# A recurrent gate and a 32-expert feed-forward layer on one core: stores among loads, one statistics call per step, and a fifth set of result buffers

## The chip, the cores and the metric
The kernel runs on one core of a Trainium2 chip. The metric is the device time of one execution in microseconds, lower being better; given is the median of several executions. The profile and the trace come from one further execution with the hardware profiler on.

## The reference, cut to what matters
x is 4 x 2048 tokens of 256 numbers, so 8192 tokens.

```python
xn = layernorm(x)
# s: recurrent layer of xn
combined = xn @ W_in + b_in               # 256 embedding columns, 8 state inputs
gate = sigmoid(combined @ W_g + b_g)      # 8 gates per token
state[t] = gate[t] * state[t-1] + (1 - gate[t]) * state_in[t]      # a scan along 2048 tokens
s = concat(embed, states) @ W_out + b_out
# y: 32 experts, each token goes to 4 of them, at most 1280 tokens each
scores = softmax(xn @ wg.T)               # 8 groups of 4 experts, 4 groups kept, then the top 4
y[token] += weight * ((silu(xe @ w1) * (xe @ w3)) @ w2)            # for each expert's tokens xe
# z: one expert that all tokens go through
z = (silu(xn @ sw1) * (xn @ sw3)) @ sw2
out = x + s * silu(y + z)
```

## The kernel before
**Units of work.** The tokens are 64 tiles of 128. A pair is two tiles (256 rows), the unit in which every matrix product is done. A group is two pairs (four tiles, 512 tokens), the unit of the loads of x, of the layer norm's statistics and of the routing. There are 32 pairs and 16 groups.

**First stage, 32 steps p = 0 to 31.** A step works on one pair. PE's loop is at L1174: it turns the next pair's rows (`transposes`, L1056), multiplies the pair by the shared expert's first matrix, then does `meanwhile` (L1180 to L1200), then the third matrix. `meanwhile` adds the states' part of s (`add_states`, L1135), forms the gates' input of the next pair (`gate_inputs(p + 1)`, L1145 to L1158), which needs the low halves `xl` of that pair from DVE (L1698, waited for at L1148), places a group's rows (`positions`), finishes the pair before (`down(p - 1)`, L1090 to L1092, its result is z), and forms the state's inputs and the logits (`s_inputs(p + 1)`, L1123 to L1125). In step 29 it also counts the early rows (`cnt_early`, L1196 to L1200).

DVE's loop is at L1891. A step is, in this order: `gate_act(p-1)` (L1704), `xlow(p+1)` (L1698, which `gate_inputs(p + 1)` waits for), `act_low` (L1708); then in even steps the end of the routing of the group before, the recurrence of the next pair (`recurrence`, L1713 and L1721; it waits for ACT's tanh of the gate inputs), `states_low` (L1727, waits for ACT's `states_high`, L1448), `statistics`, and the routing's begin; in odd steps `statistics`, the recurrence, the group's routing (top groups, top experts) and `states_low`. `statistics(g)` (L1601) is four BN statistics instructions (L1607) and four aggregates (L1610). Calls of the early steps: group 3 in step 0 and group 4 behind its states, groups 5 and 6 behind the states of step 2 (L1917 to L1919), group 7 at the end of step 3 (L1949 to L1951), group g + 6 ahead of the recurrence of step 2g + 1 for g = 2 to 9.

ACT copies z out of PSUM into a single buffer `yw` (`take_z`, L1424 to L1431) and waits for the store of the z before (L1430). It comes before the next `states_high` and before the normalised rows of the next tiles in ACT's order.

POOL's order (L895 to L903): for each of the 16 groups, once `dest_idx` (DVE, L1817) is there, 16 indirect DMAs that scatter rows of x with their routing weights to `slot_rows`, the expert's table in DRAM (L900). Behind all of them come the adds (L883): two indirect DMAs per pair that add an expert's results to `y_sum` (z's table in DRAM).

SP's order is written out by hand (L529 to L840). Loads of x by group: 0 to 5 early, 6 to 9, then 10 to 15 (L558 and L559), each with a wait for the load eight groups before; behind all of these a loop that stores z of pairs 0 to 29 (L561 to L568), then the early experts' rows (`load_early`, L673), which need the counts of L1199 and the scatters up to a group.

**Expert stage.** 142 pairs q, PE some 4.7 us each. Experts 0 to 5 start early with 17 pairs while the last groups are still being routed; from expert 6 on each has a section of four pairs and, where it has over 1024 rows, a fifth (DVE's `section`, L2022). A result, scaled by its weight, is written by DVE (`take_y_before`, L1969 to L1978) to a result buffer and added by POOL. A set is five buffers; there are four sets, A to D, carved from the storage of x and others (L203 to L208), used in turn by `y_set` (L229 to L231). Before DVE writes to a buffer it waits until the add that used it has landed: `free_wait` (L2008) for slots 0 to 3, and for a fifth result the sum of all fifths of experts up to two before (L2031). x, whose storage the sets took, is loaded again between the sections (`load_x_again`, L667, L757 to L772), for the last stage, which computes `out`.

DVE runs the sections of experts 6 to 9 as straight code, those of 10 to 17 as two turns of a loop of four sections (L2063 to L2069), 18 and 19 straight, the rest as a loop of two. POOL's code has the same form (L978 to L990).

Of the kernel before, what the change touches and what calls it, by code (L numbers as in the profile page):

```python
# [8 lines left out]
U32 = mybir.dt.uint32  # L9
# [5 lines left out]
D = 256  # L15
# [8 lines left out]
E = 32  # L24
# [40 lines left out]
SETS = 4  # L65
CYCLE_END = 18
# [15 lines left out]
def build(nc, x, w_in, b_in, w_g, b_g, w_out, b_out, wg, w1, w2, w3, sw1, sw2, sw3, out):  # L82
    ctx = ExitStack()
    with ctx:
# [120 lines left out]
        y_idx_early = x_space(2 * (2 * SET + EXTRA_Y)).bitcast(U32)  # L205
        assert words[0] <= X_KEPT * CHUNK * D
        y_flat += [x_words[:, c * CHUNK * D:(c + 1) * CHUNK * D] for c in range(X_KEPT, X_KEPT + SET)]
        y_flat += set_c + set_d + extra_y  # L208
# [10 lines left out]
        SET_A, SET_B, SET_C, SET_D, EXTRA = (n * SET for n in range(SETS + 1))  # L219
# [122 lines left out]
        added = [[sem(f"added{n}_{slot}") for slot in range(PAIRS)] for n in range(SETS)]  # L342
# [99 lines left out]
        def set_uses(e):  # L442

            return (e - FIRST) // SETS if e < CYCLE_END else (e - CYCLE_END) // 2 + (CYCLE_END - FIRST) // SETS

# [74 lines left out]
        def _(sp):  # L520
# [38 lines left out]
            for g in range(10, GROUPS):  # L559
                load_x(g)  # L560
# [6 lines left out]
            with sp.Fori(0, A_PAIRS - 2) as q:  # L567
                store_z(q)  # L568
# [105 lines left out]
            for q in range(2):  # L674
                load_early(q)
            sp.wait_ge(xn_ready, N // P - 2 * GT)
# [83 lines left out]
            sp.wait_ge(first_added, first_adds(CYCLE_END - 6))  # L760
            with sp.Fori(CYCLE_END, CYCLE_END + 4) as e:
                section(e)
                load_x_again(e - FIRST)
            sp.wait_ge(first_added, first_adds(CYCLE_END + 1))
            with sp.Fori(CYCLE_END + 4, CYCLE_END + 9) as e:
                section(e)
                for n in range(2):
                    load_x_again(e * 2 - (CYCLE_END + 4) * 2 + CYCLE_END + 4 - FIRST + n)
            section(CYCLE_END + 9)
            load_x_again(X_KEPT - 1)  # L770
            with sp.Fori(CYCLE_END + 10, E - 2) as e:
                section(e)  # L772
# [71 lines left out]
        def _(pool):  # L844
# [133 lines left out]
            for e in range(FIRST, FIRST + SETS):  # L978
                section(e, y_set(e), y_set(e - 1) if e > FIRST else None, set_uses(e - 1) + 1)
            with pool.Fori(0, (CYCLE_END - FIRST) // SETS - 1) as i:  # L980
                for n in range(SETS):
                    section(i * SETS + FIRST + SETS + n, n * SET, (n - 1) % SETS * SET, i + 1 if n == 0 else i + 2)
            for e in range(CYCLE_END, CYCLE_END + 2):
                section(e, y_set(e), y_set(e - 1), set_uses(e - 1) + 1)
            with pool.Fori(0, (E - 2 - CYCLE_END - 2) // 2) as i:
                section(i * 2 + CYCLE_END + 2, SET_B, SET_A, i + 4)
# [23 lines left out]
        def _(pe):  # L1010
# [163 lines left out]
            for p in range(A_PAIRS):  # L1174
# [5 lines left out]
                def meanwhile():  # L1180
                    add_states(p, i)
                    if has_next:
# [13 lines left out]
                    if p == A_PAIRS - 3:  # L1196
                        pe.wait_ge(early_seen, GROUPS - 2)
                        pe.wait_ge(pos_taken, GROUPS - 2)
                        mm(cnt_early, ones[:, 0:1], seen_early[:, 1:GROUPS - 1, :].rearrange("p g e -> p (g e)"),  # L1199
                           start=True, stop=True).then_inc(cnt_ready, 1)  # L1200
# [373 lines left out]
        def _(ve):  # L1574
# [316 lines left out]
            for p in range(A_PAIRS):  # L1891
# [13 lines left out]
                if i == 0:  # L1905
# [24 lines left out]
                else:  # L1930
# [3 lines left out]
                    if p == A_PAIRS - 3:  # L1934
                        count_early()
                        mark_late()
                    if has_next:
                        if 2 <= g < 10:
# [3 lines left out]
                        recurrence(p + 1, 1 - i, g % BATCH_GROUPS == BATCH_GROUPS - 1)  # L1942
                    if has_next:
# [189 lines left out]
```

## Time and profile before

| | |
|---|---|
| median of 3 runs | 1074.14 us (1073.2 to 1076.17) |
| the profiled execution | 1077.56 us |
| its span, first to last instruction | 1075.8 us |
| mean granted clock of PE | 0.972 |
| PE / DVE / ACT / POOL busy | 93% / 72% / 51% / 68% |

The share of busy time is a mean over stages. The stages lie, in the profiled execution, at 0 to 102.6 us (set-up and the first groups), to 404 us (the rest of the first stage and the early experts beside the scatters), to 510.4 us (early experts and expert 6 to 8 beside the adds), to 1000 us (the other experts), and to 1075.8 us (the rows beyond the sections and `out`). "PEclk" is the granted clock of PE: 1.00 is 2.4 GHz, 0.50 is 1.2 GHz.

### The profile page before, as it was taken

How to read it: one execution, taken by the hardware profiler on the slowest of the kernel's cores; microseconds unless marked ns; L12 is line 12 of the kernel's file. 1: busy time of each engine (PE TensorE's matmuls, PEld its weight loads, DVE VectorE, ACT ScalarE, POOL GpSimd, SP SyncE). 2: the span in 40 equal slices, each digit the busy share in tenths (PEclk: the TensorE clock that was granted, in tenths of full speed). 3: DMA queues.
4: the chain of work that ended last, by engine and by line, in shares of the span. 5: the costliest groups of instructions: out<-in, count | busy, mean ns of one | idle time of the engine just before them, and what ended most of it. 6: DMA issues, size and time to landing. Idle time of an engine off the chain costs nothing.

```text
span 1075.8 us, 29677 instructions
## 1 busy us (share of the span) xinstructions
PE 1001.6 (93%) x8031; PEld 955.9 (89%) x8031; DVE 775.6 (72%) x2475; ACT 549.5 (51%) x1039; POOL 726.3 (68%) x572
## 2 busy tenths in 40 slices
PE   7879999998979997997999999999999999999965
PEld 6878898888879997997999999999999999999822
DVE  6778898887868874765677667767667777767674
ACT  4657786877654442443344344444444444444444
POOL 3066777777777776777888887666666666665440
PEclk8889999999999999999999999999999999999997
DMA  9933433443357878997899988988788988878879
GB/s 257 285 120 130 145 141 141 143 145 140 141 159 250 261 230 169 207 181 144 161 174 201 191 167 170 199 184 179 168 201 184 211 191 190 170 141 179 217 204 340
DMA packets 179346, 199.28 MB, mean 185 GB/s; under 512 B 20737, under 2 KB 171058, under 8 KB 179250
## 3 DMA queue, kind: packets, MB, share of 16 engines
q1 hardware_dynamic: 124992, 126.70, 39.6%
q0 software_dynamic: 53664, 71.50, 35.0%
q8 instruction: 34, 0.56, 0.2%
q14 instruction: 62, 0.51, 0.2%
q10 hardware_dynamic: 594, 0.01, 0.0%
HBM read 96.89 MB, written 104.90 MB: 188 GB/s over the span
## 4 chain that ended last, share of the span: by engine, by line
PE 55%; POOL 19%; issue 12%; DMA 6%; DVE 3%; ACT 2%; SPq 1%; POOLq 1%; DVEq 0%; ACTq 0%
POOL slot_rows L900 16%; PE h L1072 10%; PE h L1074 10%; PE h L1073 10%; PE yb L1090 5%; PE yb L1092 5%; PE yb L1091 5%; PE xt L1056 5%; POOL y_sum L883 4%; DMA y_sum<-y_more,y_idx 2%; DMA x_all<-slot_rows 1%; DMA y_sum<-x_all 1%; DMA y_sum<-yw,y_idx 1%; DVE s_all L2103 1%; DMA w_hl<-y_sum 1%
## 5 line engine op out<-in xcount | busy, mean ns | idle before, releaser
L1072 PE MATMUL h<-xh,w_hl 128*128 (+1 forms) x1392 | 410.4, 295 | 3.6 <-DVE xl L1698 2.0
L1074 PE MATMUL h<-xl,w_hl 128*128 (+1 forms) x1392 | 393.5, 283 | 0.0
L1073 PE MATMUL h<-xh,w_hl 128*128 (+1 forms) x1392 | 392.1, 282 | 0.0
L1422 ACT ACTIVATE acth<-act 128x512 fp32r<-128x512 f32 x174 | 109.9, 632 | 346.3 <-PE yb L1092 306.0
L1072 PEld LDWEIGHTS h<-xh,w_hl 128*128 128x128 f32 x1392 | 264.0, 190 | 5.5 <-issue 5.0
L1073 PEld LDWEIGHTS h<-xh,w_hl 128*128 128x128 f32 x1392 | 264.3, 190 | 0.0
L1074 PEld LDWEIGHTS h<-xl,w_hl 128*128 128x128 f32 x1392 | 263.5, 189 | 0.0
L1708 DVE TENSOR_TENSOR actl<-act,acth 128x512 fp32r<-128x512 f32 x174 | 120.6, 693 | 173.7 <-ACT acth L1422 173.2
L1090 PE MATMUL yb<-w_hl,acth 128*128 128x256 f32 x692 | 199.7, 289 | 8.6 <-DVE x_all L1977 6.3
L883 POOL DMA_INDIRECT y_sum<-x_all,y_idx x98 | 156.0, 1592 | 69.1 <-DVE x_all L1977 42.2
L1092 PE MATMUL yb<-w_hl,actl 128*128 128x256 f32 x692 | 197.5, 285 | 0.0
L1091 PE MATMUL yb<-w_hl,acth 128*128 128x256 f32 x692 | 197.1, 285 | 0.0
L900 POOL DMA_INDIRECT slot_rows<-rows,dest_idx x128 | 130.3, 1018 | 86.4 <-DVE dest_idx L1817 48.3
L883 POOL DMA_INDIRECT y_sum<-y_more,y_idx x82 | 130.5, 1592 | 59.8 <-DVE y_more L1977 32.5
L900 POOL DMA_INDIRECT slot_rows<-x_all x128 | 132.5, 1035 | 39.0 <-issue 38.4
L883 POOL DMA_INDIRECT y_sum<-x_all x78 | 124.6, 1597 | 33.3 <-issue 17.2
L1090 PEld LDWEIGHTS yb<-w_hl,acth 128*128 128x128 f32 x692 | 132.9, 192 | 15.4 <-issue 15.3
L1416 ACT ACTIVATE act<-h 128x512 f32<-128x512 f32 x174 | 104.1, 599 | 81.0 <-DVE actl L1708 76.8
L1698 DVE TENSOR_TENSOR xl<-xt,xh 128x512 f32 (+1 forms) x174 | 119.1, 685 | 20.3 <-ACT xh L1410 18.0
L1092 PEld LDWEIGHTS yb<-w_hl,actl 128*128 128x128 f32 x692 | 133.1, 192 | 0.0
L1091 PEld LDWEIGHTS yb<-w_hl,acth 128*128 128x128 f32 x692 | 132.8, 192 | 0.0
L1704 DVE TENSOR_TENSOR act<-act,h 128x512 f32<-128x512 f32 x174 | 117.8, 677 | 3.9 <-PE h L1074 3.0
(253 smaller groups left out, 1606.0 us busy)
## 6 DMA issues: line engine op xcount, KB each, us to landing
rows<-slot_rows SPq DMA_DIRECT2D x122, 289.0 KB, 4.2
raw<-L_ffn_w SPq DMA_DIRECT2D x99, 256.0 KB
slot_rows<-rows SPq DMA_DIRECT2D x32, 289.0 KB
x_all<-L_attn_x SPq DMA_DIRECT2D x16, 512.0 KB, 9.3
x_all<-L_attn_x SPq DMA_DIRECT2D x32, 256.0 KB
out<-s_all SPq DMA_DIRECT2D x32, 256.0 KB, 3.7
y_sum<-yw SPq DMA_DIRECT2D x31, 256.0 KB
x_all<-slot_rows SPq DMA_DIRECT2D x20, 289.0 KB, 4.5
```

The source lines that it names most:

```text
L883: pool.indirect_dma_start(y_dram, bass.IndirectOffsetOnAxis(y_index(buf, t), 0), y_out[buf][:, t, :], None, bounds_check=token_bound, oob_ ...
L900: pool.indirect_dma_start(slot_table, bass.IndirectOffsetOnAxis(dest_idx[slot][:, t, k:k + 1], 0), rows[slot][:, t, :], None, bounds_check ...
L1072: mm(out, high, xh[:, k, cols], start=(k == 0), stop=False)
L1073: mm(out, low, xh[:, k, cols], start=False, stop=False)
L1074: ins = mm(out, high, xl[:, k, cols], start=False, stop=(k == KD - 1))
L1090: mm(dst, acth[:, c:c + P], wts[:, 4, k, :], start=(k == 0), stop=False)
L1091: mm(dst, acth[:, c:c + P], wts[:, 5, k, :], start=False, stop=False)
L1092: ins = mm(dst, actl[:, c:c + P], wts[:, 4, k, :], start=False, stop=(k == KD - 1))
L1422: av(acth[:, :], act[:, :], ACT.Copy).then_inc(acth_ready, 2)
L1698: v.tensor_tensor(xl[:, :, cols], xt[:, :].rearrange("p (k t) -> p k t", k=KD), xh[:, :, cols].bitcast(F32), ALU.subtract).then_inc(xl_rea ...
L1704: v.tensor_tensor(act[:, :], act[:, :], h3[:, :], ALU.mult).then_inc(act_ready, 1)
L1708: v.tensor_tensor(actl[:, :], act[:, :], acth[:, :].bitcast(F32), ALU.subtract).then_inc(actl_ready, 2)
```

## The change
1. **SP.** The stores of z(0), z(1) and z(2) are put ahead of the loads of x of groups 10, 12 and 14. `load_early(0)` comes ahead of the store of z(28), `load_early(1)` ahead of that of z(29).
2. **DVE, statistics.** One call per step: group 4 in step 0 as before, group 5 in step 1 ahead of `recurrence(2)`, group 6 in step 2, group 7 in step 3 ahead of `recurrence(4)`.
3. **Step 29.** DVE's `count_early` and `mark_late` move behind `recurrence(30)`; PE's `cnt_early` moves from the end of `meanwhile` to right behind `add_states`.
4. **Result buffers.** A fifth set, E, of five buffers in the storage of x's chunks 0 to 4, used by expert 7 alone, which waits for no add. Experts 8 to 19 go round B, C, D, A; from 20 on B and A in turn, as before. One more primer DMA (a 16th) runs at POOL's start.
5. **Loops and loads.** Experts 6 to 11 are straight code, 12 to 19 two turns of a loop of four, 20 and 21 straight, then a loop of two. x's chunks 5 to 12 are loaded again behind sections 6 to 13, chunks 0 to 4 behind 14 to 18, 13 to 15 behind 19 to 21, then two each.

```diff
-SETS = 4
-CYCLE_END = 18
+SETS = 5
+CYCLE = 4
+CYCLE_START = 8
+CYCLE_END = 20
+KEPT_START = 14
...
-            return (SET_A, SET_B, SET_C, SET_D)[(e - FIRST) % SETS] if e < CYCLE_END else (SET_B, SET_A)[e % 2]
+            if e < CYCLE_START:
+                return (SET_A, SET_E)[e - FIRST]
+            return CYCLE_SETS[(e - CYCLE_START) % CYCLE] if e < CYCLE_END else (SET_B, SET_A)[e % 2]
...
-            for g in range(10, GROUPS):
-                load_x(g)
...
-            with sp.Fori(0, A_PAIRS - 2) as q:
+            for g in range(10, GROUPS):
+                if g % 2 == 0:
+                    store_z(g // 2 - 5)
+                load_x(g)
+            with sp.Fori(3, A_PAIRS - 4) as q:
                 store_z(q)
...
             for q in range(2):
                 load_early(q)
+                store_z(A_PAIRS - 4 + q)
...
-            with sp.Fori(FIRST, CYCLE_END) as e:
+            with sp.Fori(FIRST, KEPT_START) as e:
+                section(e)
+                load_x_again(e - FIRST + SET)
+            sp.wait_ge(first_added, first_adds(KEPT_START - SET))
+            with sp.Fori(KEPT_START, KEPT_START + SET) as e:
+                section(e)
+                load_x_again(e - KEPT_START)
...
                 def meanwhile():
                     add_states(p, i)
+                    if p == A_PAIRS - 3:
+                        pe.wait_ge(early_seen, GROUPS - 2)
+                        pe.wait_ge(pos_taken, GROUPS - 2)
+                        mm(cnt_early, ones[:, 0:1], seen_early[:, 1:GROUPS - 1, :].rearrange("p g e -> p (g e)"),
+                           start=True, stop=True).then_inc(cnt_ready, 1)
...
-                    if g == 0:
-                        statistics(4)
-                    if g == 1:
-                        statistics(5)
-                        statistics(6)
+                    if g in (0, 1):
+                        statistics(4 + 2 * g)
...
-                    if p == A_PAIRS - 3:
-                        count_early()
-                        mark_late()
                     if has_next:
+                        if g in (0, 1):
+                            statistics(5 + 2 * g)
...
                         recurrence(p + 1, 1 - i, g % BATCH_GROUPS == BATCH_GROUPS - 1)
+                    if p == A_PAIRS - 3:
+                        count_early()
+                        mark_late()
...
                     if g == 1:
-                        statistics(7)
                         variances(norm_chunk(g + 3))
...
-                if e < FIRST + SETS:
+                if e == FIRST + 1:
+                    return None, 0
+                if e < CYCLE_START + CYCLE - 1:
```

## Rows read from the trace of the kernel before

**Rows 1.** The page: busy time by engine, then the chain that ended last by engine.
```profile
PE 1001.6 (93%) x8031; PEld 955.9 (89%) x8031; DVE 775.6 (72%) x2475; ACT 549.5 (51%) x1039; POOL 726.3 (68%) x572
PE 55%; POOL 19%; issue 12%; DMA 6%; DVE 3%; ACT 2%; SPq 1%; POOLq 1%; DVEq 0%; ACTq 0%
```

**Rows 2.** Windows: us, sum, busy PE, PEld, DVE, ACT, POOL, PEclk, DMA, GB/s.
```profile
102.60:404.00 301.40, 283.23 (x2353) 268.11 (x2350) 244.88 (x1007) 199.33 (x398) 232.88 (x225) 0.99 0.52 172
404.00:510.40 106.40, 93.78 (x777) 93.01 (x777) 64.80 (x169) 40.05 (x71) 77.29 (x48) 0.97 0.87 176
510.40:1000.00 489.60, 487.42 (x4103) 486.81 (x4104) 347.03 (x894) 215.57 (x383) 350.64 (x221) 0.99 0.86 180
```

**Rows 3.** Timeline of POOL: start, duration, instruction, idle time before it and releaser.
```profile
50.64 1.25 POOL L900 DMA_INDIRECT slot_rows<-rows,dest_idx  x1 [38.89 <-DVE dest_idx L1817]
...
77.32 1.29 POOL L900 DMA_INDIRECT slot_rows<-rows,dest_idx  x1 [6.10 <-DVE dest_idx L1817]
...
101.32 0.98 POOL L900 DMA_INDIRECT slot_rows<-rows,dest_idx  x1 [3.34 <-DVE dest_idx L1817]
...
398.95 1.07 POOL L900 DMA_INDIRECT slot_rows<-x_all  x1 [0.30 <-issue]
...
504.92 1.55 POOL L883 DMA_INDIRECT y_sum<-y_more,y_idx  x1 [0.30 <-issue]
```

**Rows 4.** Groups of POOL's instructions from 102.6 to 400.1 us, by line.
```profile
L900 POOL DMA_INDIRECT slot_rows<-x_all x128 | 132.5, 1035 | 39.0 <-issue 38.4 <-DVE x_all L1817 0.3 <-DVE x_all L1977 0.3
```

**Rows 5.** Timeline of PE after 400 us, then of DVE at 509 us.
```profile
408.94 1.12 PE L1056 MATMUL xt<-ident,x_all 128*128 128x128 f32 x4 [5.20 <-DMA x_all<-slot_rows]
...
510.33 0.55 PE L1090 MATMUL yb<-w_hl,acth 128*128 128x256 f32 x1 [6.27 <-DVE x_all L1977]
...
509.00 0.15 DVE L1976 CAST x_all<-meta 128x1 uint32 x1 [6.68 <-DMA y_sum<-y_more,y_idx]
```

**Rows 6.** Timeline of PE: the end of down(1), then the gate inputs of three early steps.
```profile
50.98 0.41 PE L1092 MATMUL yb<-w_hl,actl 128*128 128x256 f32 x1
...
60.41 0.37 PE L1155 MATMUL gb<-xh,wgh 128*48 128x256 f32 x1 [2.83 <-issue]
...
73.07 0.29 PE L1155 MATMUL gb<-xh,wgh 128*48 128x256 f32 x1 [3.72 <-issue]
...
93.12 0.29 PE L1155 MATMUL gb<-xh,wgh 128*48 128x256 f32 x1 [0.85 <-DVE xl L1698]
```

**Rows 7.** Timeline of DVE, 39 to 77 us, in order of time.
```profile
39.54 0.41 DVE L1713 SCALAR_TENSOR_TENSOR raw<-raw,gb 16x256 f32<-16x256 f32 x1 [1.15 <-ACT raw L1442]
...
54.67 1.41 DVE L1607 BATCH_NORM_STATS2 stats<-x_all 128x6 f32<-128x256 f32 x4
...
56.60 1.41 DVE L1607 BATCH_NORM_STATS2 stats<-x_all 128x6 f32<-128x256 f32 x4
...
63.35 0.41 DVE L1713 SCALAR_TENSOR_TENSOR raw<-raw,gb 16x256 f32<-16x256 f32 x1 [2.14 <-ACT raw L1442]
...
67.73 0.41 DVE L1727 TENSOR_TENSOR state_hl<-raw,state_hl 16x256 fp32r<-16x256 f32 x1 [1.03 <-ACT state_hl L1448]
...
69.62 1.40 DVE L1607 BATCH_NORM_STATS2 stats<-x_all 128x6 f32<-128x256 f32 x4
```

**Rows 8.** Windows of the early steps, columns as in rows 2.
```profile
60.40:63.90 3.50, 3.49 (x17) 3.42 (x18) 1.11 (x3) 2.86 (x6) 2.58 (x4) 0.51 0.31 110
74.10:80.90 6.80, 6.80 (x41) 6.58 (x41) 3.75 (x16) 3.09 (x7) 2.97 (x3) 0.50 0.23 77
82.00:100.00 18.00, 16.98 (x144) 15.91 (x143) 15.14 (x67) 14.05 (x29) 12.32 (x13) 1.00 0.39 140
```

**Rows 9.** Timeline of ACT, then of SP's queue, at the second copy of z.
```profile
52.81 0.60 ACT L1431 ACTIVATE yw<-yb 128x512 f32<-128x512 f32 x1 [3.78 <-DMA y_sum<-yw]
...
47.31 18.14 SPq L564 DMA_DIRECT2D y_sum<-yw  x3
```

**Rows 10.** Timeline of DVE behind the end of its loop of four sections.
```profile
617.99 0.20 DVE L1966 COPY meta<-rows 128x66 f32 x1 [2.71 <-issue]
```

More of the change, by code:

```diff
@@ L217, in y_index @@
             return y_idx_early[:, column:column + 1]
-        SET_A, SET_B, SET_C, SET_D, EXTRA = (n * SET for n in range(SETS + 1))
+        SET_A, SET_B, SET_C, SET_D, SET_E, EXTRA = (n * SET for n in range(SETS + 1))
+        CYCLE_SETS = (SET_B, SET_C, SET_D, SET_A)
         BEHIND_FIFTH, BEHIND_LAST = EXTRA + 1, EXTRA + 2
@@ L341, in build @@
         y_ready = sem("y_ready")
-        added = [[sem(f"added{n}_{slot}") for slot in range(PAIRS)] for n in range(SETS)]
+        added = [[None] + [sem(f"added{n}_{slot}") for slot in range(1, PAIRS)] for n in range(SETS)]
         first_added = sem("first_added")
@@ L442, in set_uses @@
         def set_uses(e):
-            return (e - FIRST) // SETS if e < CYCLE_END else (e - CYCLE_END) // 2 + (CYCLE_END - FIRST) // SETS
+            if e < CYCLE_START:
+                return 0
+            if e < CYCLE_END:
+                return (e - CYCLE_START) // CYCLE + (y_set(e) == SET_A)
+            return (e - CYCLE_END) // 2 + (CYCLE_END - CYCLE_START) // CYCLE + e % 2
         def first_adds(e):
@@ L977, in _ @@
                 pool.reg_mov(fifth_behind, 1)
-            for e in range(FIRST, FIRST + SETS):
+            for e in range(FIRST, CYCLE_START + CYCLE):
                 section(e, y_set(e), y_set(e - 1) if e > FIRST else None, set_uses(e - 1) + 1)
-            with pool.Fori(0, (CYCLE_END - FIRST) // SETS - 1) as i:
-                for n in range(SETS):
-                    section(i * SETS + FIRST + SETS + n, n * SET, (n - 1) % SETS * SET, i + 1 if n == 0 else i + 2)
+            with pool.Fori(0, (CYCLE_END - CYCLE_START) // CYCLE - 1) as i:
+                for n in range(CYCLE):
+                    section(i * CYCLE + CYCLE_START + CYCLE + n, CYCLE_SETS[n], CYCLE_SETS[n - 1], i + 2)
             for e in range(CYCLE_END, CYCLE_END + 2):
@@ L1195, in meanwhile @@
                         positions(g - 1)
-                    if p == A_PAIRS - 3:
[L1197 to L1200, printed above, removed]
                 up(p, w_hl[1], region(i), meanwhile)
@@ L2028, in body @@
                     if slot == PAIRS:
-                        if isinstance(e, int) and e < FIRST + SETS:
+                        if isinstance(e, int) and e < CYCLE_START + CYCLE - 1 and e != FIRST + 1:
                             ve.wait_ge(*waits(slot))
@@ L2062, in _ @@
                 pair(PAIRS, 1, (FIRST - 2, SET_A + PAIRS, fifth_added, 32), slot=PAIRS)
-            for e in range(FIRST, FIRST + SETS):
+            for e in range(FIRST, CYCLE_START + CYCLE):
                 section(e, (e + 1) % 2, y_set(e), lambda slot, e=e: free_wait(e, slot), FIRST - 2 if e == FIRST else None)
-            with ve.Fori(0, (CYCLE_END - FIRST) // SETS - 1) as i:
-                for n in range(SETS):
-                    e = i * SETS + FIRST + SETS + n
-                    section(e, (n + 1) % 2, n * SET, lambda slot, e=e, n=n: (first_added, first_adds(e - SETS))
-                            if slot == 0 else (added[n][slot], slot_adds(slot, i + 1)))
+            with ve.Fori(0, (CYCLE_END - CYCLE_START) // CYCLE - 1) as i:
+                for n, home in enumerate(CYCLE_SETS):
+                    e = i * CYCLE + CYCLE_START + CYCLE + n
+                    section(e, (n + 1) % 2, home, lambda slot, e=e, home=home: (first_added, first_adds(e - CYCLE))
+                            if slot == 0 else (added[home // SET][slot], slot_adds(slot, i + (2 if home == SET_A else 1))))
             for e in range(CYCLE_END, CYCLE_END + 2):
@@ L2075, in _ @@
                     section(e, 1 - n, home, lambda slot, e=e, home=home: (first_added, first_adds(e - 2)) if slot == 0 else
-                            (added[home // SET][slot], slot_adds(slot, i + 4)))
+                            (added[home // SET][slot], slot_adds(slot, i + (5 if home == SET_A else 4))))
             uses = set_uses(E - 1) + 1
```

24 lines of the change are left out of this document (10 added, 14 removed).

## The prediction

> **What bounds the kernel now.** I read the page first [rows 1]: PE is busy for 93% of the span, and on the chain that ended last PE has 55% and POOL 19%, nearly all of it scatters of one line. So there are two bounds, one after the other, and the windows by stage tell where. From 510.4 to 1000 us PE is busy for 487.42 of 489.6 us: nothing but PE's own work counts there. From 102.6 to 404 us it is busy for 283.23 of 301.4 us, and from 404 to 510.4 us for 93.78 of 106.4 us [rows 2]: there somebody else leads.
>
> That is POOL. Its timeline shows the scatters of group 0 from 50.64 us, of group 1 from 77.32 us, of group 2 from 101.32 us, each after an idle time that DVE's `dest_idx` ended (38.89, 6.10, 3.34 us); the last of group 15 begins at 398.95 us after an idle time of only 0.30 us [rows 3]. From group 2 on there are 14 groups of 16 scatters, 224 of them; at 1.035 us each [rows 4] and 0.30 us between them that is 299 us, and from 101.3 us to the last one's end at 400.0 us there are 298.7. So POOL doesn't pause once between group 2's dispatch and 400 us. The adds follow, and they too are back to back when the second half of a pair is added at 504.92 us [rows 3].
>
> Now who waits for POOL? PE, twice. At 408.94 us it has stood 5.20 us for a row load that needs the last scatter; at 510.33 us it has stood 6.27 us for DVE, which had stood 6.68 us for an add into `y_sum` (the one of 504.92 us), before it could take expert 8's fifth result [rows 5]. That is the wait of L2031, for all fifths of experts up to 6. Behind it PE never waits for POOL again. So the end is group 2's dispatch, plus POOL's fixed work to 508.8 us, plus PE's fixed work behind 510. What PE alone saves between 102 and 510 us makes those two waits longer and is given back; what brings group 2's dispatch forward passes to the end.
>
> **The change part by part.** *Statistics, the part that counts.* Up to 100 us, DVE's chain from the states through the routing decides. PE stands 2.83 us ahead of the gate inputs of pair 4 at 60.41 us and 3.72 us ahead of those of pair 5 at 73.07 us [rows 6], both times until DVE has made `xl`. In DVE's timeline [rows 7] the calls of groups 5 and 6 begin at 54.67 and 56.60 us, between the states and `xl`. One of them leaves: −1.93 us.
>
> The call of group 7 stands at 69.62 us, again between the states and `xl`: it leaves too, at the price of the other call, start to start: −1.93 us. Where it goes, ahead of `recurrence(4)`, DVE stands 2.14 us for ACT at 63.35 us [rows 7]; 1.93 us of work fit into that, so it costs nothing there. If that cover were gone, it would cost its 1.93 us.
>
> Between the two lies a wait of 1.03 us for ACT's high states at 67.73 us [rows 7], which come behind ACT's copy of z, hence behind PE's `down(2)`. PE does those products from 60.40 to 63.90 us at a granted clock of 0.51, the lower level of 1.2 GHz, right behind its idle time of 2.83 us [rows 8]. With 1.93 us less in front of it, that idle time is 0.9 us. The nearest row for such a short one is 93.12 us, 0.85 us idle [rows 6], and the clock of the window around it is 1.00 [rows 8]. At 2.4 GHz the 3.49 busy us take half, so the high states come up to 1.75 us earlier and the wait of 1.03 us nearly goes: I take −0.85, leaving the 0.2 us that DVE commonly waits for ACT; bounds −1.03 and 0.
>
> Against it: the call of group 5 goes into step 1, ahead of `recurrence(2)`, where DVE waits 1.15 us at 39.54 us [rows 7]: 1.93 − 1.15 = +0.78 us (bounds 0.78 and 1.93). That delay reaches the dispatch of group 0, where it costs nothing while group 1's comes 5 us earlier: POOL had 6.10 us to spare between the two [rows 3]. On the way to step 2 it meets the next part.
>
> *Stores of z among the loads.* ACT's second copy of z begins at 52.81 us, after 3.78 us in which it ended up waiting for the store of the first, which SP issued at 47.31 us [rows 9] behind six loads of x of 512 KB each; PE had finished `down(1)` at 51.39 us [rows 6]. DVE's states of step 2 wait for ACT behind that copy. With the store ahead of the loads the copy is released by PE: 51.39 + 0.78 = 52.17 us, 0.64 us before 52.81. So the +0.78 is swallowed here, and up to 0.64 us are won on top; bounds +0.78 (should the store be no earlier) and −0.64. I take −0.3 for both together, half of what is won, since DVE's other work of step 2 comes 0.78 us later too. The loads of groups 10 to 15 come later, but the statistics of group 10 are taken only in step 9, behind 100 us. SP stands at three stores instead of running through; behind it are those loads alone.
>
> Sum for group 2's dispatch: −1.93 − 1.93 − 0.85 − 0.3 = −5.0 us, so 101.32 becomes 96.3. Bounds: −3.86 + 0.78 = −3.1 with the 0.85 gone and the 0.78 kept, −3.86 − 1.03 − 0.64 = −5.5 with all at their best. Two things could cap it. POOL must be free: group 0's scatters begin at 50.64 + 0.78 and, like group 1's, take 101.32 − 3.34 − 77.32 = 20.7 us, so POOL is free for group 1 from 72.1 us, just before 77.32 − 5.0 = 72.3; that is over at 93.0 us, before 96.3. And steps 4 to 6 have to keep their length, since PE is busy for 16.98 of the 18 us from 82 to 100 us [rows 8]; I take them unchanged.
>
> *Step 29, early rows.* `cnt_early` without its wait behind `meanwhile`, and early rows ahead of the last stores, can save PE a few us before 404. POOL is scattering then without a pause, so I cost them at nothing: they lengthen the wait that stood at 408.94 us. If POOL weren't the bound there, they would add to the gain.
>
> *Fifth set.* The wait at 510.33 us is for the fifths' adds [rows 5], not for a set to come free; expert 8's fifth still waits so (L2031 is unchanged). From there on PE has 2.2 us of idle time in all of 489.6 us [rows 2], so buffers that come free earlier buy nothing: 0. The changed reloads of x run behind sections on SP in that same stretch; as long as PE stays full they cost nothing. If an add were late where a reload or a set waits, the wait would show in PE.
>
> *Loops.* DVE stood for 2.71 us with nothing that the profile shows [rows 10], behind the turn of its loop of four sections; the new code has one such turn too, two experts later: 0.
>
> In all −5.0 us: 1074.14 − 5.0 = **1069.1 us**. The rows come from an execution of 1077.56 us, 3.4 us above the median; the same difference would make a profiled execution of about 1072.5. The forecast's own range, by the bounds, is 1068.6 to 1071.0.
>
> **The rivals.** *R1, the clock gives more.* PE's idle time at pair 5's gate inputs doesn't vanish: `xl` comes 5.0 us earlier, PE's own work up to 4.0 us (1.93 and 0.3, and up to 1.75 from the clock), so of 3.72 us some 2.7 remain. In before, 3.72 us were followed by 6.80 us at 0.50 [rows 8], which cost PE half of that, 3.4 us. If the shorter stand isn't followed by a slow stretch, steps 4 to 6 shrink by 3.4, and the gain is 5.0 + 3.4 = 8.4, capped by POOL, which is free for group 2 at 93.0 + 0.3: 8.0, 1066.1 us. Against it: the 2.83 us at 60.41 were followed by a slow stretch.
> The Trainium skill ("TensorE: Matmul & The Clock Gate", Part 1: The HAM clock gate) says that the low clock is the state an idle engine falls into and that the same kernel shows 6, 11 or 14 slow matmuls from run to run; by that the time would be drawn between this rival and the forecast in each run. The one trace of before can't show it.
>
> *R2, the clock gives less.* The slow stretch behind pair 4's gate inputs stays in spite of the shorter idle time, and another of 3.4 us falls into steps 5 or 6: the sum is then −3.1 + 1.7 = −1.4, 1072.7 us (1071.0 to 1074.1). For it speaks that PE's short idle times are many; against it, the window at 1.00 around the 0.85 us.
>
> *R3, the fifth set removes the wait at 510.33.* Then 6.27 us more go, and with them the half-speed stretch that follows a long stand, some 2: 1074.1 − 5.0 − 6.3 − 2 = 1060.8 us. Against it is the releaser: an add into `y_sum` from `y_more` [rows 5], a set which E doesn't replace. That the change doesn't do what it says would look like this rival's opposite, and is the forecast without it.
>
> *R4, slower.* DVE's straight code now holds experts 10 and 11. If the branch over a fifth that isn't there stops DVE as its loop's turn does (2.71 us [rows 10]), PE, which has nothing in reserve behind 510, loses some 2 us and up to 1.7 by a slow stretch: 3.7 us each. Two such stops cost 7.4, the change ends at +2.4, 1076.5 us; it decides from the second stop on, and a third makes it 1080.2. Against it: the same branches lay inside the loop of before, and only its turn shows such an idle time.
> The Trainium skill ("Runtime: NRT & Kernel Launch", Instruction fetch mechanics) says that a taken branch to code that isn't held forces a fetch before execution goes on. The row of 2.71 us agrees; that a short forward branch does it no row here shows.
>
> **How the numbers follow.** Forecast 0.54, R1 0.18, R2 0.16, R3 0.04, R4 0.08. The range 1065.9 to 1072.8 takes the forecast with its bounds, nearly all of R1 and two thirds of R2: about 0.8. A measurement of this kernel can tell about 0.3% from no change, 3.2 us. Faster than 1070.9: forecast (less 0.02 at its upper bound), R1 and R3, 0.74; within: R2, that 0.02 and half of R4, 0.22; slower: the other half of R4, 0.04.
>
> **What would show it.** In the trace of after: POOL's first scatter of group 2 near 96.3 us and its last near 394.0; no idle time of PE over 1 us at pair 4's gate inputs, some 2.7 us at pair 5's; the two waits of rows 5 still there, the first one longer, the second one ending near 505.3 us; ACT's second copy of z released by PE. The prediction is wrong if group 2's dispatch moves by less than 3 us or more than 6, if the shift at group 2 isn't found again at 510 us, or if PE idles anew behind it.

## The result, and the profile after

The changed kernel takes 1068.19 us (median of 20 runs, 1063.86 to 1075.76) beside 1073.32 us for the kernel before (20 runs on the same chips): a ratio of 0.995 with a 95% interval of 0.9933 to 0.9966, so 5.1 us less. The forecast was 5.0 us less. The profiled execution has a span of 1069.6 us, 6.2 us under that of before.

First the page's busy times and the windows of the stages, here bounded by group 2's first scatter, the end of the last scatter and the end of PE's second stand (in rows 2 the middle bound, 404 us, lies 4 us behind the end of the last scatter). The columns are those of rows 2: us, sum, PE, PEld, DVE, ACT, POOL, PEclk, DMA, GB/s.

```profile
PE 997.1 (93%) x8031; PEld 952.3 (89%) x8031; DVE 774.9 (72%) x2475; ACT 548.9 (51%) x1039; POOL 726.4 (68%) x573
...
94.00:390.90 296.90, 282.80 (x2353) 268.17 (x2352) 245.34 (x1006) 199.20 (x398) 228.94 (x224) 0.99 0.53 173
390.90:504.30 113.40, 95.22 (x787) 94.24 (x786) 65.54 (x171) 40.64 (x72) 80.66 (x50) 0.95 0.85 168
504.30:1000.00 495.70, 491.61 (x4131) 490.61 (x4132) 350.02 (x903) 217.13 (x386) 354.01 (x222) 0.99 0.86 180
```

Little was saved in work: PE is busy for 997.1 us against 1001.6. In the last of these stretches PE is again busy all but 4 us. The change lies in when things begin. POOL's timeline (start, duration, instruction, idle time before and its releaser) answers to rows 3:

```profile
50.70 1.25 POOL L916 DMA_INDIRECT slot_rows<-rows,dest_idx  x1 [38.47 <-DVE dest_idx L1833]
...
71.97 0.98 POOL L916 DMA_INDIRECT slot_rows<-rows,dest_idx  x1 [0.30 <-issue]
...
93.97 0.98 POOL L916 DMA_INDIRECT slot_rows<-rows,dest_idx  x1 [0.80 <-DVE dest_idx L1833]
...
389.92 0.98 POOL L916 DMA_INDIRECT slot_rows<-x_all  x1 [0.30 <-issue]
```

Group 0 begins where it did (50.70 us for 50.64). Group 1 comes at 71.97 us instead of 77.32, now without a pause (0.30 us), group 2 at 93.97 instead of 101.32: 7.35 us earlier, with 0.80 us of idle time left of 3.34. POOL is now occupied from the first dispatch on. The last scatter is 9.0 us earlier. Next PE's idle times at the gate inputs and at its waits for others, answering to rows 6 and 5, and the DVE instruction behind the second wait:

```profile
57.15 0.29 PE L1171 MATMUL gb<-xh,wgh 128*48 128x256 f32 x1 [0.22 <-issue]
...
66.90 0.29 PE L1171 MATMUL gb<-xh,wgh 128*48 128x256 f32 x1 [2.00 <-issue]
...
396.91 0.90 PE L1072 MATMUL xt<-ident,x_all 128*128 128x128 f32 x3 [4.85 <-DMA x_all<-slot_rows]
...
504.14 0.55 PE L1106 MATMUL yb<-w_hl,acth 128*128 128x256 f32 x1 [11.92 <-DVE x_all L1991]
...
502.81 0.15 DVE L1990 CAST y_idx<-meta 128x1 uint32 x1 [12.34 <-DMA y_sum<-y_more,y_idx]
```

The idle time at pair 4's gate inputs is 0.22 us (2.83 before), at pair 5's 2.00 us (3.72). PE's stand of 5.20 us at 408.94 has become one of 4.85 us, but 12 us earlier; the one of 6.27 us at 510.33 has become 11.92 us and ends only 6.2 us earlier. So 12 us arrive at 397 us, and half of them are waited for again at 504.14 us, behind DVE, which stood 12.34 us for the landing of an add.

### The profile page after: what moved, and what is told of

Read it like the earlier page. It is cut to its first block, busy times and chain, and to the rows that moved or that the text cites. A ratio compares the mean times of both kernels' runs of the same rounds, so it can differ in the third digit from the quotient of the medians.

```text
span 1069.6 us, 29639 instructions
## 1 busy us (share of the span) xinstructions
PE 997.1 (93%) x8031; PEld 952.3 (89%) x8031; DVE 774.9 (72%) x2475; ACT 548.9 (51%) x1039; POOL 726.4 (68%) x573
## 3 DMA queue, kind: packets, MB, share of 16 engines
HBM read 96.89 MB, written 104.90 MB: 189 GB/s over the span
## 4 chain that ended last, share of the span: by engine, by line
PE 54%; issue 3%; DMA 3%; POOL 2%; DVE 1%; ACT 0%; DVEq 0%; POOLq 0%; SPq 0%; ACTq 0%
PE h L1088 11%; PE h L1090 11%; PE h L1089 11%; PE yb L1108 5%; PE yb L1106 5%; PE yb L1107 5%; PE xt L1072 5%; DMA y_sum<-y_more,y_idx 2%; POOL y_sum L899 1%; POOL slot_rows L916 1%; DVE s_all L2119 0%; DMA x_all<-slot_rows 0%; DMA w_hl<-y_sum 0%; DMA slot_rows<-x_all 0%; ACT acth L1438 0%
## 5 line engine op out<-in xcount | busy, mean ns | idle before, releaser
L1106 PE MATMUL yb<-w_hl,acth 128*128 128x256 f32 x692 | 199.1, 288 | 14.3 <-DVE x_all L1991 11.9
L899 POOL DMA_INDIRECT y_sum<-x_all,y_idx x88 | 140.4, 1595 | 66.9 <-DVE x_all L1991 41.8
L899 POOL DMA_INDIRECT y_sum<-x_all x90 | 144.4, 1604 | 41.7 <-issue 21.4
L899 POOL DMA_INDIRECT y_sum<-y_more,y_idx x80 | 127.3, 1592 | 55.9 <-DVE y_more L1991 31.1
```

The costliest lines, as they stand in the source:

```text
L899: pool.indirect_dma_start(y_dram, bass.IndirectOffsetOnAxis(y_index(buf, t), 0), y_out[buf][:, t, :], None, bounds_check=token_bound, oob_ ...
L1106: mm(dst, acth[:, c:c + P], wts[:, 4, k, :], start=(k == 0), stop=False)
```

## The experiments

Each kernel was timed in five rounds beside the kernel before on the same chip. "From group 0" below means the time of an event less that of group 0's first scatter, since this first event itself lies between 49.3 and 54.3 us in the profiled executions (last section).

### The parts of the first stage

**Statistics alone.**
```diff
-                    if g == 0:
-                        statistics(4)
-                    if g == 1:
-                        statistics(5)
-                        statistics(6)
+                    if g in (0, 1):
+                        statistics(4 + 2 * g)
...
                     if has_next:
+                        if g in (0, 1):
+                            statistics(5 + 2 * g)
...
                     if g == 1:
-                        statistics(7)
```


> The kernel before with the statistics calls of groups 5 and 7 moved as in the change, and nothing else. Theory (group 2's dispatch sets the end): its first scatter comes at 97.4 us instead of 101.32 (-1.93 - 1.93 - 0.85, and +0.78 in step 1, which is not swallowed without the early store of z), and the time falls by about 4 us. Rival (the statistics only move idle time, and the stores of z or the fifth set carry the gain): first scatter within 1 us of 101.3, time unchanged.

Measured: 1068.37 us, ratio 0.9949 (0.9925 to 0.9972). ACT's second copy of z and POOL's groups 1 and 2:

```profile
51.47 0.60 ACT L1431 ACTIVATE yw<-yb 128x512 f32<-128x512 f32 x1 [3.16 <-DMA y_sum<-yw]
...
71.18 1.29 POOL L900 DMA_INDIRECT slot_rows<-rows,dest_idx  x1 [0.70 <-issue]
...
95.18 0.98 POOL L900 DMA_INDIRECT slot_rows<-rows,dest_idx  x1 [3.34 <-DVE dest_idx L1817]
```

The copy is still released by the store (a DMA), as it was to be. Group 2 comes at 95.18 us, 45.3 us from group 0 (49.91 us) where before needed 50.7: 5.4 us earlier, 1.5 more than expected, and the time moves by 5.5 us by the ratio (1073 x 0.0051). The theory holds, its size was low.

**Stores of z alone.**
```diff
-            for g in range(10, GROUPS):
-                load_x(g)
...
+            for g in range(10, GROUPS):
+                if g % 2 == 0:
+                    store_z(g // 2 - 5)
+                load_x(g)
```


> The kernel before with only the stores of z(0) to z(2) among the loads of x. Theory: ACT's second copy of z no longer waits for the store and comes up to 1.4 us earlier (from 52.81 to the end of PE's product, 51.4), step 2 shortens by that, and group 2's first scatter and the time fall by 0.5 to 1.4 us, less than can be told from no change. Rival (the stores are the lever): 3 us or more at the dispatch and in the time.

Measured: 1072.36 us, ratio 0.9975 (0.9949 to 1.0).

```profile
49.79 0.60 ACT L1432 ACTIVATE yw<-yb 128x512 f32<-128x512 f32 x1 [2.06 <-PE yb L1093]
...
98.44 0.98 POOL L901 DMA_INDIRECT slot_rows<-rows,dest_idx  x1 [3.34 <-DVE dest_idx L1818]
```

The copy is now released by PE's product instead of the store, and group 2 comes 49.1 us from group 0 (49.32 us) instead of 50.7: 1.6 us. The time's interval holds 0 to 5.5 us and can't tell that from nothing. By the dispatch the stores are not the lever.

**Both.** The two diffs together.

> The kernel before with the moved statistics and the early stores of z, without the moves of step 29, the early rows, the fifth set and the loads of x. Theory: this is all that reaches the end. Group 2's first scatter between 94 and 96.5 us (94 was seen with the whole change), and the same time as the whole change, 5 us less than before. Rival (the later parts carry some of it): the dispatch moves as much, but the time falls by 2.5 us or less.

Measured: 1066.28 us, ratio 0.9936 (0.9912 to 0.9959); the whole change has 0.995. The first scatters of groups 0 and 2:

```profile
54.27 1.25 POOL L901 DMA_INDIRECT slot_rows<-rows,dest_idx  x1 [42.55 <-DVE dest_idx L1818]
...
96.89 0.98 POOL L901 DMA_INDIRECT slot_rows<-rows,dest_idx  x1 [0.30 <-issue]
```

Group 2's is at 96.89 us, outside the expected 94 to 96.5, because group 0's came at 54.27 in this execution; from group 0 it is 42.6 us, 8.1 less than before. That is near the least there can be: two groups of 16 scatters with no pause between (three of the later kernels have 42.1 us). All that can be told of what the change brings to the end is in these two edits.

**The whole first stage, without the fifth set.** Both, and the moves of step 29 and of the early rows:
```diff
-            with sp.Fori(3, A_PAIRS - 2) as q:
+            with sp.Fori(3, A_PAIRS - 4) as q:
                 store_z(q)
...
             for q in range(2):
                 load_early(q)
+                store_z(A_PAIRS - 4 + q)
...
                     add_states(p, i)
+                    if p == A_PAIRS - 3:
+                        pe.wait_ge(early_seen, GROUPS - 2)
+                        pe.wait_ge(pos_taken, GROUPS - 2)
+                        mm(cnt_early, ones[:, 0:1], seen_early[:, 1:GROUPS - 1, :].rearrange("p g e -> p (g e)"),
+                           start=True, stop=True).then_inc(cnt_ready, 1)
```


> The whole change of the first stage (statistics, stores of z, step 29, early rows), with the four sets, the loops and the loads of x of before. Theory: the time of the whole change, 5 us less than before; PE reaches the early experts several us earlier than with the statistics and the stores alone, and its wait near 505 us is longer by as much. Rival 1 (step 29 and early rows reach the end): 3 us or more below the kernel with the statistics and the stores alone. Rival 2 (the fifth set gives or costs something): more than 2 us off the whole change.

Measured: 1066.49 us, ratio 0.9947 (0.9924 to 0.9971). PE's two stands without these moves (first two lines) and with them (last two):

```profile
403.44 0.90 PE L1057 MATMUL xt<-ident,x_all 128*128 128x128 f32 x3 [5.70 <-DMA x_all<-slot_rows]
...
501.48 0.36 PE L1091 MATMUL yb<-w_hl,acth 128*128 128x256 f32 x1 [2.38 <-DVE x_all L1976]
```

```profile
393.40 0.90 PE L1058 MATMUL xt<-ident,x_all 128*128 128x128 f32 x3 [4.80 <-DMA x_all<-slot_rows]
...
495.48 0.55 PE L1092 MATMUL yb<-w_hl,acth 128*128 128x256 f32 x1 [5.65 <-DVE x_all L1977]
```

From group 0 the row load comes at 349.2 us without them and at 343.6 with them: 5.6 us won. The later stand is 2.38 us without and 5.65 with: 3.3 of them waited for again, and in the time nothing is left that can be told (1066.28 and 1066.49). Rival 1 falls, as in the forecast.

**The fifth set alone.** The set, the loops and the loads of x of the change, with the first stage of before.

> The fifth set, the loops and the loads of x of the change, with the first stage of before. Theory (no set is waited for): the time of before within 2 us, the wait before expert 8's fifth result still there, released by an add, of 5 to 12 us. Rival (the fifth set frees buffers that are waited for): the wait is gone or falls under 3 us, and the time falls by 5 us.

Measured: 1072.02 us, ratio 0.9996 (0.9972 to 1.002). The stand is there, but shorter than expected:

```profile
507.36 0.36 PE L1104 MATMUL yb<-w_hl,acth 128*128 128x256 f32 x1 [1.44 <-DVE x_all L1991]
```

It is 1.44 us here, 5.2 to 11.9 us in the other kernels that keep the wait (2.38 with both edits). So the rival's first sign came in, a stand of under 3 us, and its second, a time 5 us lower, didn't. Two things made the stand shorter in this execution: it ends 3.0 us earlier than in before (POOL's last scatter is 1.3 us earlier, and from there to the landing of the add that is waited for there are 1.7 us less), and PE arrives at it 1.9 us later (505.92 us for 504.06). The adds vary as much between the other kernels (see "What was lost on the way"). That the set had no part in it isn't shown by this one execution; the time, the same as before within 0.3%, shows that it is worth nothing that can be told, and rival R3 of the forecast falls with it.

### Does group 2's dispatch set the end?

The same extra work was put on DVE at one of two places, 12 statistics instructions one after the other, at the beginning of step 5 or (p == 17) of step 17:
```diff
+                if p == 5:
+                    for n in range(12):
+                        v.bn_stats(spent[:, :], x_all[:, 0, :]).then_inc(spent_step, 1)
+                        ve.wait_ge(spent_step, n + 1)
```


> The whole change with some 5 us of extra work on DVE at the beginning of step 5, ahead of group 2's dispatch. Theory (group 2's dispatch sets the end): the first scatter of group 2 comes some 4.5 us later (POOL had under 1 us of idle time there), and the time is 4 to 5 us above the whole change's, about that of before. Rival (PE's own chain sets the end, and the first stage's waits are swallowed later): within 2 us of the whole change.

> The same extra work on DVE at the beginning of step 17, when POOL has scatters queued. Theory: POOL doesn't notice; PE reaches the early experts 5 us later and stands as much less in its two waits for POOL (4.85 and 11.92 us in the whole change); the time is the whole change's within 2 us. Rival (PE's chain sets the end): 4 to 5 us above it.

Measured: in step 5 1074.52 us, ratio 1.0016 (0.9994 to 1.0038), so 6.3 us above the whole change's 1068.19; in step 17 1067.77 us, ratio 0.9945 (0.9917 to 0.9972), the whole change's. First step 5, then step 17, POOL and PE of each:

```profile
98.59 0.98 POOL L918 DMA_INDIRECT slot_rows<-rows,dest_idx  x1 [5.19 <-DVE dest_idx L1835]
...
403.06 0.90 PE L1074 MATMUL xt<-ident,x_all 128*128 128x128 f32 x3 [7.40 <-DMA x_all<-slot_rows]
...
504.90 0.55 PE L1108 MATMUL yb<-w_hl,acth 128*128 128x256 f32 x1 [5.62 <-DVE x_all L1997]
```

```profile
91.92 0.98 POOL L918 DMA_INDIRECT slot_rows<-rows,dest_idx  x1 [0.30 <-issue]
...
184.84 0.42 PE L1173 MATMUL gb<-xh,wgh 128*48 128x256 f32 x1 [5.68 <-issue]
...
400.44 0.91 PE L1074 MATMUL xt<-ident,x_all 128*128 128x128 f32 x3 [5.22 <-DMA x_all<-slot_rows]
...
502.13 0.55 PE L1108 MATMUL yb<-w_hl,acth 128*128 128x256 f32 x1 [5.24 <-DVE x_all L1997]
```

In step 5 POOL stands 5.19 us before group 2 (0.80 in the whole change). In step 17 PE itself stands 5.68 us at 184.84 us while POOL goes on, and the end doesn't see it. PE's two stands take it up instead, 10.5 us together where the whole change has 16.8. This is the most direct evidence: 5 us ahead of group 2's dispatch cost the end all of themselves, 5 us behind it cost nothing.

One thing in it doesn't fit. From group 0 (51.73 us) group 2 comes at 46.9 us with the delay in step 5, 3.6 us later than in the whole change and still 3.8 us earlier than before. By that the time should lie 4 us above the whole change and 4 us under before; the median lies 6.3 above the one and not under the other. The profiled execution was among the fastest of this kernel's twelve (1071.08 us), and what the slower ones have in addition is not shown.

### What the stand near 504 us is worth

The wait of a fifth result is for all fifths up to two experts before, in whichever buffers. For experts 7 to 10 the fifth buffers (E, B, C and D) have had no fifth in them, so these results need only their own buffer's add. (Expert 7's fifth result waits in this way too; that its set "waits for no add", as the list of the change has it, holds for its other four results.)
```diff
                         free, landed = fifth_added, fifth_adds(ve.snap(ahead_fifths))
+                        if isinstance(e, int) and FIRST < e < CYCLE_START + CYCLE - 1:
+                            free, landed = None, 0
```


> The whole change, and the fifth results of experts 7 to 10 wait for the add that used their own buffer alone, no longer for the fifths' adds of the experts before, which these buffers had no part in. Theory (that wait is the last place where POOL holds PE): the stand of PE near 504 us (11.92 us with the whole change, 5 to 6 in the kernels without the fifth set) is gone, no other wait for an add takes its place, and the time falls by 5 to 10 us below the whole change. Rival (POOL is behind anyway, the next result waits for its set instead): a wait of several us for an add behind 504 us, and a gain under 3 us.

Measured: 1056.34 us (1054.96 to 1062.41), ratio 0.9838 (0.9809 to 0.9868), 11.9 us under the whole change. PE's stand at the row load, and its next one of over a microsecond:

```profile
398.00 0.90 PE L1072 MATMUL xt<-ident,x_all 128*128 128x128 f32 x3 [4.84 <-DMA x_all<-slot_rows]
...
644.61 0.58 PE L1088 MATMUL h<-xh,w_hl 128*128 x1 [3.71 <-DVE xl L1714]
```

Between 398 and 644.61 us PE doesn't stand any more for an add. The rival (POOL is behind anyway) falls.

The same on the kernel before, experts 7 to 9:

> The kernel before, and the fifth results of experts 7 to 9 wait for the add that used their own buffer alone. Theory: the stand of 6.27 us at 510.33 us goes, and the time falls by 6 to 12 us; group 2's late dispatch still holds PE at its row load near 409 us, so the kernel stays 5 to 10 us above the whole change with the same edit (1056.3). Rival (behind the first stage all that the change does comes from the adds, and with those waits gone its first-stage part is worth nothing): within 2 us of 1056.3.

Measured: 1066.95 us, ratio 0.9934 (0.991 to 0.9959): 7 us under before, and 10.6 us above the whole change with the same edit, just over the range. With that wait the change was worth 5.1 us; without it, twice as much.

Then the statistics and the stores alone, on the kernel before with the fifths apart:

> The kernel before with the moved statistics, the early stores of z and the fifth results apart, without the moves of step 29, the early rows and the fifth set. With the waits for the fifths in place, step 29 and the early rows were worth nothing (1066.3 without them, 1066.5 with them). Theory (they were given back at the stand near 505 us): with that stand gone they count; PE's wait for the row load near 400 us ends some 3 to 5 us later than with them, counted from group 0's first scatter (346.3 with them), and the time is 2 to 5 us above 1056.3. Rival (they are hidden behind the scatters in any case): within 1.5 us of 1056.3.

Measured: 1057.82 us, ratio 0.9878 (0.9839 to 0.9916). By the medians that is 1.5 us above 1056.34, by the ratios 4.3, and the intervals overlap. PE's row load came 348.4 us from group 0, 2.2 later than with step 29 and the early rows, less than the 3 to 5 expected. Whether these moves count once the wait is gone stays open.

### The loop's turn

```diff
-            with ve.Fori(0, (CYCLE_END - CYCLE_START) // CYCLE - 1) as i:
+            for i in range((CYCLE_END - CYCLE_START) // CYCLE - 1):
```


> The whole change, the fifth results apart as before, and DVE's loop of four sections (experts 12 to 19) written out as straight code. Theory (the turn of the loop stops DVE, 4.4 us, and PE 3.7 us at 644 us): that stand is gone with the slow stretch behind it, and the time falls by 3.5 to 7 us to about 1051. Rival (longer straight code stops DVE at its branches over missing fifths instead): one or more new stands of PE of 2 to 4 us for DVE, and no gain.

> The whole change with DVE's loop of four sections (experts 12 to 19) written out as straight code, the waits as in the change. Theory: PE stands no more at 658 us (3.66 us in the whole change), and the time falls by 3.5 to 5.5 us below the whole change. Rival as for the kernel with the fifths apart: no gain, other stands for DVE.

Measured: with the fifths apart 1052.39 us (1049.45 to 1055.99), ratio 0.9801 (0.9773 to 0.983); with the waits of the change 1063.47 us, ratio 0.9897 (0.9861 to 0.9934). So 4.0 and 4.7 us less, by the medians, than with the loop; there are six runs of each straight kernel, and in both pairs the intervals of the ratios overlap a little. What went, in the whole change, is PE's stand at 658 us and DVE's idle time ahead of it:

```profile
656.70 0.20 DVE L1980 COPY meta<-rows 128x66 f32 x1 [4.77 <-issue]
...
658.15 0.38 PE L1088 MATMUL h<-xh,w_hl 128*128 x1 [3.66 <-DVE xl L1714]
```

In the straight kernels PE has no idle time of over 0.8 us behind 409 us (with the fifths apart) or behind 500 us, its stand for POOL (with the waits of the change), until 996 us. The rival (straight code stops at the branches over missing fifths) falls. The kernel with both edits is the fastest of all, 2% under before.

## Why the prediction was right, and where it was not

**The bound: right.** The end follows group 2's dispatch: with 5 us of DVE's work ahead of it the time rises by 6.3 us; the same work 12 steps later does nothing. The edits that move the dispatch (5.4, 1.6 and 8.1 us from group 0) move the time by 5.5, 2.7 (not to be told from 0) and 6.9 us, by the ratios; those that don't (step 29, early rows, fifth set) leave it, as long as the wait near 504 us is there.

**The sum: right in sign and order, its terms too small.** The forecast was −5.0 us at the dispatch with bounds of −3.1 and −5.5; measured are −7.4. That is also over the 6 us from which on the prediction calls itself wrong. So the agreement of the time, 5.1 us for 5.0, is better than that of the parts, and in part luck: of the 7.4 us at the dispatch only 6.2 are left at 504 us and in the span of the profiled execution, and 5.1 in the medians. Here are DVE's states of step 2 in before, then DVE and ACT in the changed kernel, answering to rows 7 and 9:

```profile
54.23 0.42 DVE L1727 TENSOR_TENSOR state_hl<-raw,state_hl 16x256 fp32r<-16x256 f32 x1 [3.21 <-ACT state_hl L1448]
```

```profile
51.54 0.60 ACT L1447 ACTIVATE yw<-yb 128x512 f32<-128x512 f32 x1 [2.94 <-PE yb L1108]
...
52.96 0.42 DVE L1743 TENSOR_TENSOR state_hl<-raw,state_hl 16x256 fp32r<-16x256 f32 x1 [1.89 <-ACT state_hl L1464]
...
60.09 0.41 DVE L1729 SCALAR_TENSOR_TENSOR raw<-raw,gb 16x256 f32<-16x256 f32 x1 [0.41 <-ACT raw L1458]
...
63.42 0.41 DVE L1743 TENSOR_TENSOR state_hl<-raw,state_hl 16x256 fp32r<-16x256 f32 x1
```

- Statistics of group 7 into the wait ahead of `recurrence(4)`: as forecast, 0.41 us of 2.14 are left at 60.09 us.
- The wait for the high states, −0.85 forecast out of 1.03: gone entirely at 63.42 us.
- The copy of z: forecast at 52.17 us, released by PE; it is at 51.54 us, 2.94 us after the instruction before and released by PE. The states behind it come at 52.96 instead of 54.23, −1.3 us where −0.3 was taken. That is the term that was mis-sized most: the delay of 0.78 us was to reach PE's `down(1)` and didn't (its last product ends at 51.45 us, for 51.39). With the store alone the dispatch gains 1.6 us.
- So pair 5's gate inputs are at 66.90 us: −6.2, not −5.0.

The rest is the clock, the mechanism of rival R1. In before, 6.80 us at 0.50 followed pair 5's gate inputs [rows 8]. In the changed kernel, behind an idle time of 2.00 us, 3.40 us did:

```profile
57.00:60.50 3.50, 3.28 (x25) 3.06 (x26) 2.84 (x12) 3.44 (x7) 2.59 (x4) 1.00 0.83 301
69.10:72.50 3.40, 3.40 (x17) 3.40 (x17) 2.30 (x10) 1.43 (x4) 2.49 (x3) 0.51 0.36 139
```

And behind pair 4's gate inputs the clock is 1.00, where before had 0.51, as forecast for an idle time under 1 us. So half of R1 came in: 3.4 us less at half the clock are worth 1.7 us, and the dispatch goes from −6.2 to −7.4 us.

Whether R1 comes in differs between executions of the same first stage, and the other traces show it. The kernels with the fifths apart and with the straight loop, and those without the fifth set and with the delay in step 17, have the first stage of the change up to step 16, and PE stands 2.01 or 2.02 us at pair 5's gate inputs in all of them. In those with the fifths apart or the straight loop (three executions) 3.4 us at the low clock follow, as above, and group 2 comes 42.9 to 43.3 us from group 0. In the other two no such stretch follows, POOL has no pause at all, and group 2 comes at 42.1 us: R1 in full, with POOL as its limit. Without the fifth set:

```profile
65.38 0.29 PE L1157 MATMUL gb<-xh,wgh 128*48 128x256 f32 x1 [2.01 <-issue]
```

```profile
67.60:71.00 3.40, 3.40 (x29) 3.40 (x28) 2.67 (x11) 2.40 (x7) 2.73 (x3) 1.00 0.40 149
```

The Trainium skill ("TensorE: Matmul & The Clock Gate", Part 1: The HAM clock gate) says that the number of slow matmuls at the start of one and the same kernel differs from run to run. The 17 matmuls at the low clock in the one execution and none in the other agree, here in the middle of a kernel.

**"What PE saves between 102 and 510 us is given back": the step that failed at its first half.** I had put the stand at 408.94 us down to the last scatter, so that it would grow as PE got faster. It didn't grow: 5.20 became 4.85, and PE came through it 12 us earlier. The reason is SP. In before it issued three stores of zeros (into an expert's table, behind its rows) one after the other, then the row load:

```profile
398.26 5.35 SPq L589 DMA_DIRECT2D slot_rows<-rows  x3
404.51 0.40 SPq L601 DMA_DIRECT2D x_all<-slot_rows  x1
```

The last scatter had begun at 398.95 us [rows 3] and ended at 400.0; the row load went out only at 404.51, behind SP's own work, which follows PE and DVE. Its rows reached PE 8.9 us behind the end of the last scatter. In the changed kernel it is 6.0 us (390.90 to 396.91), the same 6.0 with the fifths apart and without the fifth set; with the statistics and the stores alone it is 10.9 us. The delay in step 17 shows the same from the other side: PE is held up, the scatters aren't, and the rows reach PE 10.8 us behind the end of the last scatter, with PE's stand at 5.22 us. So PE's savings do pass this point as long as SP is later than the scatters, and step 29 and the early rows are what made SP early. This didn't hurt the forecast of the time, because the second half of the step, the stand at 510.33 us, does take it back: 11.92 us there for 6.27.

**What was lost on the way.** The last scatter gains 9.0 us, PE at the second stand 6.2. Between them lie the adds. POOL's waits from 404 to 508 us before, then in the changed kernel (line waited, releaser: us in total, times, longest):

```profile
POOL y_sum L883 <- issue: 23.7, 42, 7.8
POOL y_sum L883 <- DMA y_sum<-x_all: 2.2, 2, 1.2
POOL y_sum L883 <- DMA y_sum<-yw,y_idx: 1.9, 1, 1.9
```

```profile
POOL y_sum L899 <- issue: 20.8, 42, 8.0
POOL y_sum L899 <- DVE x_all L1991: 4.8, 1, 4.8
POOL y_sum L899 <- DMA y_sum<-x_all: 4.6, 2, 2.4
```

All such waits together are 28.7 us before and 32.0 after (smaller lines left out). The 4.8 us bear DVE's name, but DVE had written that result 57 us before POOL added it at 481.51 us:

```profile
424.46 0.48 DVE L1991 TENSOR_SCALAR yw<-yb,meta 128x256 f32<-128x256 f32 x1
```

At this place POOL's code waits for adds of the early experts to land, and before has 3.66 us there. So these 3 us are waits for other adds to land, and POOL's work up to the second stand is not fixed, as the forecast had it. From the beginning of the last scatter to that of the add that is waited for there are 106.0 us in before, 109.0 in the changed kernel, and 103.6 to 108.2 in the eight other kernels that keep the wait. The changed kernel's 109.0 are the longest of all, with the same adds, so I don't put the 3 us down to the change. In other executions more of the 9 us may arrive.

**The fifth set at nothing: right**, 0.9996 alone. **The loop's turn at nothing: nearly.** It has moved two experts on, as forecast, but PE stood 3.66 us there instead of 2.01. That isn't chance alone: DVE's idle time behind the turn is 2.6 to 3.4 us in the seven executions with the loop of before and 3.4 to 4.8 us in the five with the loop of the change. Why it is longer isn't shown. By the medians of the straight kernels the turn as such costs 4 to 5 us, not the 2 to 3.7 which the forecast put on such a stop.

**The other rivals.** R2 (the clock gives less) fell: there are fewer slow stretches in the first 100 us, not more. R3 fell with the fifth set alone; the wait that it spoke of could be removed, but by another edit. R4 (slower) fell with the straight kernels, in which the branches over missing fifths cost PE nothing that shows.

## What to carry to other kernels

A gain is worth what gets past the last wait for the engine that is behind: here 12 us at 397 us, 5 at the end, because a fifth result waited for adds into buffers that it doesn't use. Look for the wait that gives a gain back before looking for more gains: one condition in a wait brought twice what the change did. And where a stand has several causes (a row load needs the scatters *and* the queue that issues it), compare when each of them was done, not only which the profile names.

## What the runs showed that had not been expected

Group 0's first scatter lies at 49.3 to 54.3 us in the 14 profiled executions, and the edits don't explain it: with the statistics and the stores it is 54.27, with the same edits and more 49.82. In the latest one the clock was low for longer during the set-up. The window from 8 to 25 us, in that execution and in that of the whole change:

```profile
8.20:25.30 17.10, 14.27 (x51) 9.99 (x52) 10.35 (x44) 7.37 (x19) 3.52 (x7) 0.50 1.08 295
```

```profile
8.20:25.30 17.10, 14.01 (x71) 11.48 (x70) 11.78 (x47) 9.86 (x25) 4.03 (x8) 0.72 1.08 285
```

Once POOL scatters without a pause from group 0 on, such a difference should reach the end. It fits that the two profiled executions are 5.0 us apart at group 2 (96.89 and 91.92 us) and 5.5 us in time (1067.13 and 1061.64 us), while the medians of these kernels are the same, and that the times of the changed kernel spread over 12 us (1063.86 to 1075.76). No run here changes the set-up alone.

The turn of a loop of four sections costs more than DVE's row shows: the idle time is 2.6 to 4.8 us in the traces; taken out of the changed kernels it gave 4.0 and 4.7 us of the whole kernel's time by the medians, PE being full behind it.
